# Layer 1 attention: the rotary step and the hi/lo split done in the projection's PSUM bank, row maxima over single banks in a ring of three

## What is computed

```
q, k, v = x @ wq.T, x @ wk.T, x @ wv.T           # (4, 1024, 512) each, as 16 heads of 32
q, k = apply_rope(q, k, sin, cos)                # rotates the first 16 of the 32 columns of a head
att = softmax(q k^T / sqrt(32))                  # over the 1024 keys of the batch entry
y = (att v).reshape(4, 1024, 512)
```

## Time and profile before

| | us |
|---|---|
| median of three runs | 3529.43 (3527.44 to 3536.01) |
| the profiled execution, its own time | 3538.25 |
| its span in the profile | 3536.5 |
| PE, PEld busy | 3178.8, 2231.9 |
| DVE, ACT, POOL busy | 2400.1, 1662.3, 1501.5 |
| mean granted TensorE clock | 0.96 |

### The profile page before, as it was taken

The page is one execution under the profiler, slowest core; times in us unless marked ns, Lnnn a source line. Parts: engine busy times, 40 slices in busy tenths (PEclk is TensorE's granted clock), DMA queues, the critical chain, the costliest instruction groups (busy, mean ns, idle before and its releaser), DMA issues. The chain is left out here.

```text
span 3536.5 us, 53506 instructions
## 1 busy us (share of the span) xinstructions
PE 3178.8 (90%) x16548; PEld 2231.9 (63%) x16548; DVE 2400.1 (68%) x3422; ACT 1662.3 (47%) x3006; POOL 1501.5 (42%) x1085
## 2 busy tenths in 40 slices
PE   5999999919999996999999989999999939999999
PEld 4766666617888885655555555555555418888887
DVE  4455555478888884788888888888888844444444
ACT  2211121106777774566666666666666622222222
POOL 1000000033333331377777777777777732112111
PEclk9999999959999998899999999999999969999999
DMA  2000000031222223111111111111111032122121
GB/s 83 25 24 24 30 24 24 18 113 66 90 89 89 89 78 127 60 51 54 54 55 55 54 55 50 54 54 49 54 55 54 20 150 75 60 74 68 65 74 48
DMA packets 97104, 215.26 MB, mean 61 GB/s; under 512 B 11408, under 2 KB 27792, under 8 KB 96400
## 3 DMA queue, kind: packets, MB, share of 16 engines
q1 hardware_dynamic: 95472, 210.14, 17.6%
q10 hardware_dynamic: 1440, 2.76, 0.2%
HBM read 162.54 MB, written 50.33 MB: 60 GB/s over the span
## 5 line engine op out<-in xcount | busy, mean ns | idle before, releaser
L1102 POOL TENSOR_TENSOR l_attn_summed<-l_attn_summed,l_attn_probs 128x1024 f32<-128x1024 f32 x372 | 884.8, 2402 | 161.0 <-ACT l_attn_probs L1170 160.7
L1259 DVE TENSOR_REDUCE l_attn_maxima<-l_attn_ps_max 128x2 f32<-128x1024 f32 x512 | 608.9, 1210 | 127.9 <-PE l_attn_ps_max L1367 125.3
L1170 ACT ACTIVATE l_attn_probs<-l_attn_ps_sc 128x512 f32<-128x512 f32 x1024 | 578.7, 601 | 217.7 <-PE l_attn_ps_sc L1323 200.2
L1323 PE MATMUL l_attn_ps_sc<-l_attn_q_st,l_attn_k_st 128*128 128x512 f32 x1024 | 451.9, 454 | 15.4 <-ACT l_attn_probs L1170 12.6
L70 PE MATMUL l_ffn_ps_gu<-l_ffn_w_gu,l_ffn_xt 128*128 128x512 f32 (+1 forms) x1536 | 345.6, 378 | 47.0 <-DMA l_ffn_xt<-xt_chunks 47.0
L1367 PE MATMUL l_attn_ps_max<-l_attn_k_st,l_attn_q_st 96*128 96x512 f32 x1024 | 352.9, 428 | 28.4 <-DVE l_attn_maxima L1259 28.3
L1510 POOL TENSOR_TENSOR l_ffn_mixed<-l_ffn_gate,l_ffn_up 128x512 f32<-128x512 f32 (+1 forms) x96 | 115.2, 1199 | 522.6 <-DVE l_ffn_up L1559 519.0
L70 PEld LDWEIGHTS l_ffn_ps_gu<-l_ffn_w_gu,l_ffn_xt 128*128 128x128 f32 x1536 | 279.7, 189 | 87.6 <-DMA l_ffn_xt<-xt_chunks 48.7
L1323 PEld LDWEIGHTS l_attn_ps_sc<-l_attn_q_st,l_attn_k_st 128*128 128x128 f32 x1024 | 193.9, 194 | 222.0 <-ACT l_attn_probs L1170 139.1
L1308 PE MATMUL l_attn_ps_y<-l_attn_probs,l_attn_v 128*32 128x512 f32 x2048 | 286.1, 632 | 16.5 <-issue 12.3
L61 PE MATMUL l_attn_ps_prep<-l_attn_wqkv_hi,l_attn_xt 128*128 (+1 forms) x1016 | 271.2, 348 | 31.8 <-DMA l_attn_xt<-xt_chunks 30.9
(11 more groups left out here) (232 smaller groups left out, 6584.7 us busy)
## 6 DMA issues: line engine op xcount, KB each, us to landing
l_attn_xt<-xt_chunks SPq DMA_DIRECT2D x128, 512.0 KB, 3.3
xt_chunks<-l_ffn_xt SPq DMA_DIRECT2D x32, 512.0 KB, 2.8
l_ffn_xt<-xt_chunks SPq DMA_DIRECT2D x32, 512.0 KB, 3.4
l_attn_xin<-in_x SPq DMA_DIRECT2D x32, 256.0 KB, 2.7
s<-l_attn_s_sb SPq DMA_DIRECT2D x32, 256.0 KB, 2.0
l_ffn_xa<-in_x SPq DMA_DIRECT2D x32, 256.0 KB, 2.6
l_ffn_xb<-in_x SPq DMA_DIRECT2D x32, 256.0 KB, 2.9
l_ffn_s_sb<-s SPq DMA_DIRECT2D x32, 256.0 KB, 3.6
```

Source lines behind the costliest of these rows:

```text
L1102: eng.tensor_tensor(total[:, :, :], old[:, :, :], probs[u % RING][:, :, :], ALU.add).then_inc(adds_with(g, u)[0], 1)
L1170: act.activation(probs[u % RING][:, i, :], ps_sc[i][:, :, :].rearrange("p a n -> p (a n)"), ACT.Exp, scale=ATT_SCALE).then_inc(exp_done, 1)
L1259: dve.tensor_reduce(maxima[:, j, h:h + 2, half:half + 1], ps_max[bank][:, :, :], AX.X, ALU.max).then_inc(max_read[bank], 1)
L1323: pe.matmul(ps_sc[i][:, :, :].rearrange("p a n -> p (a n)"), k_st[p][:, h, P * kt:P * kt + P], q_st[p][:, h, DIM * qb:DIM * qb + DIM], sta ...
```

## The change

1. **Banks.** `ps_max` goes from two tiles of two banks to three of one bank. The bank that comes free is `ps_proj`, for projections alone; `ps_prep` keeps q, k, den and turn. `ps_y` is declared in another shape.
2. **The rotary step in PSUM.** ACT no longer copies q and k out; it copies v alone. DVE waits for that copy, forms the two sine products into `swapped`, waits for them, multiplies by the cosines in place in `ps_proj`, and adds `swapped` in place. `turned_part` and `qk` are gone. ACT's `cast` and DVE's two subtractions read the bank. The next projection waits until both subtractions of the chunk before have been done (`stacked`).
3. **The table.** `PREP_AT` becomes `(1, 6, 7)`: projection c in slot 3 of unit 2c, its q in slot 1 and its k in slot 3 of unit 2c+3. ACT's `cast` of chunk c goes from unit 2c+2 to unit 2c+1. DVE does step 2 at the head of its unit in place of the end. "turn" is one unit earlier (units 30 and 14 in place of 31 and 15), "den" one unit later.
4. **The maxima.** 64 uses of one matmul and one reduce over 512 columns in place of 32 of two matmuls and one reduce over 1024, one to a slot.
5. **In tick 0**, which has no attention half, projections use `ps_proj` and the two `ps_sc` in turn, the other preps `ps_prep` and `ps_y`.
6. SP's loads of `xt` wait for the projection itself, no longer for ACT's copy.

```diff
-    MAX_RING = 2
+    MAX_RING = 3
-        ps_prep = ps("ps_prep", [P, 4, P])
-        ps_max = [ps(f"ps_max{i}", [P, 2, DIM]) for i in range(MAX_RING)]
+        ps_proj, ps_prep = ps("ps_proj", [P, 4, P]), ps("ps_prep", [P, 4, P])
+        ps_max = [ps(f"ps_max{i}", [P, DIM]) for i in range(MAX_RING)]
-        N_MAX = CPB * HPG // 2
-        PREP_STEP, PREP_AT = 4, (0, 7, 9)
-        DEN_AT = [2 * (LAST + 5), 2 * 7]
+        N_MAX = CPB * HPG
+        PREP_STEP, PREP_AT = 4, (1, 6, 7)
+        DEN_AT = [2 * (LAST + 6), 2 * 8]
-        EARLY = 7
+        EARLY = 14
-        TURN_AT = [2 * (UNITS - 1), 2 * (LAST - 1)]
+        TURN_AT = [2 * (UNITS - 2), 2 * (LAST - 2)]
...
+        def proj_bank(m, c):
+            banks = [ps_proj] + ps_sc if isinstance(m, int) and m == 0 else [ps_proj]
+            return banks[c % len(banks)], CPB * m + c - len(banks) + 1
... sync
-                        need(sp, qk_copied, CPB * m + c - 1)
+                        need(sp, proj_done, CPB * m + c - 1)
... scalar: cast reads bank[:, 0, :] and bank[:, 1, :] in place of x
-                    if u >= 2 and u % 2 == 0 and u // 2 <= CPB and live(m, NT):
-                        cast(m, p, u // 2 - 1)
+                    if u % 2 == 1 and u // 2 < CPB and live(m, NT):
+                        cast(m, p, u // 2)
...
+                        if kind == "proj":
+                            need(act, proj_done, CPB * m + c + 1)
+                            act.activation(v[p][:, c, :], proj_bank(m, c)[0][:, 2, :], ACT.Copy).then_inc(v_copied, 1)
+                            continue
... vector, chunk
-                    need(dve, qk_copied, n + 1)
-                    (cosine product into turned_part, two sine products into swapped)
+                    need(dve, v_copied, n + 1)
+                    dve.tensor_tensor(swapped[:, :, 0:R // 2], x[:, :, R // 2:R], sc(sin_t, 0, R // 2), ALU.mult).then_inc(rope_step, 1)
+                    dve.tensor_tensor(swapped[:, :, R // 2:R], x[:, :, 0:R // 2], sc(sin_t, R // 2, R), ALU.mult).then_inc(rope_step, 1)
+                    need(dve, rope_step, S * n + 2)
+                    dve.tensor_tensor(x[:, :, 0:R], x[:, :, 0:R], sc(cos_t, 0, R), ALU.mult).then_inc(rope_step, 1)
                 elif step == 1:
                     need(dve, rope_step, S * n + 3)
+                    dve.tensor_tensor(x[:, :, 0:R], x[:, :, 0:R], swapped[:, :, :], ALU.add).then_inc(rope_step, 1)
... tensor, prepare and maximum
+                    bank, free = proj_bank(m, c)
+                    need(pe, stacked, 2 * free)
-                for i in range(2):
-                    (matmul of head h + i into dst[:, i, :])
+                pe.matmul(dst[:, :], q_st[b][0:AUG, h, P * j:P * j + P], k_st[b][0:AUG, h, DIM * half:DIM * half + DIM],
+                          start=True, stop=True).then_inc(max_done[bank], 1)
+                    per_slot = -(-len(todo) // 4)
-                        for e in todo[slot // 2::2] if slot % 2 == 0 else []:
+                        for e in todo[per_slot * slot:per_slot * (slot + 1)]:
```

More of the change, by code:

```diff
@@ L1060, in ring @@
             of_tick = lambda m: [e for e in uses if exists(m, e)]
-            before = lambda m: sum(len(of_tick(i)) for i in range(m))
-            assert len(uses) % banks == 0
+            on = lambda n, bank: (n - bank + banks - 1) // banks
             def use(m, e):
                 if isinstance(m, int):
[L1066 to L1069, removed]
+                    n = of_tick(m).index(e)
+                    return n % banks, sum(on(len(of_tick(i)), n % banks) for i in range(m)) + n // banks
+                n = uses.index(e)
+                first = sum(on(len(of_tick(i)), n % banks) for i in range(2))
+                return n % banks, on(len(uses), n % banks) * (m - 2) + first + n // banks
             return use
-        prep_use = ring([e for u in range(UNITS) for e in preps(u) if e], 1)
+        prep_use = ring([e for u in range(UNITS) for e in preps(u) if e and e[0] != "proj"], 1)
         max_use = ring([e for u in range(UNITS) for e in maxes(u)], MAX_RING)
         def prep_bank(m, e):
-            banks = [ps_prep] + ps_sc if isinstance(m, int) and m == 0 else [ps_prep]
+            banks = [ps_prep, ps_y] if isinstance(m, int) and m == 0 else [ps_prep]
             n = prep_use(m, e)[1]
             return banks[n % len(banks)] if len(banks) > 1 else ps_prep, n - len(banks) + 1
+        def proj_bank(m, c):
+            banks = [ps_proj] + ps_sc if isinstance(m, int) and m == 0 else [ps_proj]
+            return banks[c % len(banks)], CPB * m + c - len(banks) + 1
         def adds_with(g, u):
@@ L1149, in cast @@
                 n = CPB * m + c
-                x, qs, ks = qk[c % 2], q_tok[c % 2], k_tok[c % 2]
+                bank, qs, ks = proj_bank(m, c)[0], q_tok[c % 2], k_tok[c % 2]
                 if not (isinstance(m, int) and m == 0 and c < 2):
@@ L1258, in maximum @@
                 need(dve, max_done[bank], before + 1)
-                dve.tensor_reduce(maxima[:, j, h:h + 2, half:half + 1], ps_max[bank][:, :, :],
+                dve.tensor_reduce(maxima[:, j, h, half:half + 1], ps_max[bank][:, :],
                                   AX.X, ALU.max).then_inc(max_read[bank], 1)
@@ L1280, in tick @@
                     for c in range(CPB):
+                        if u == PREP_STEP * c // 2 + 2 and live(m, NT):
+                            chunk(m, p, c, 2)
                         if u == PREP_STEP * c // 2 + 1 and live(m, NT):
@@ L1287, in tick @@
                         maximum(m, a)
-                    for c in range(CPB):
-                        if u == PREP_STEP * c // 2 + 2 and live(m, NT):
-                            chunk(m, p, c, 2)
                     for qb in range(QB):
@@ L1304, in pv @@
                 need(pe, exp_done, 2 * (UNITS * g + 2 * j + 2))
+                y = ps_y[:, :, :].rearrange("p a n -> p (a n)")
+                if isinstance(g, int) and g == 0 and j == 0:
+                    need(pe, prep_read, prep_use(0, ("turn", 0))[1] + 1)
                 if kt == 0:
@@ L1336, in prepare @@
                     three_pass(pe, bank[:, 0:3, :].rearrange("p a n -> p (a n)"), lambda k: xt[b][:, 0, k, :], lambda k: xt[b][:, 1, k, :],
[L1337 to L1338 removed]
+                               cols(w_hi), cols(w_lo), KD, proj_done)
+                    return
+                bank, read_before = prep_bank(m, e)
+                need(pe, prep_read, read_before)
+                if kind == "den":
                     for pair in range(2):
```

49 lines of the change are left out of this document (17 added, 32 removed).

## The result

| | before | after |
|---|---|---|
| median, us | 3529.24 (3527.44 to 3536.01) | 3782.54 (3778.47 to 3793.26) |
| profiled execution, its own time | 3538.25 | 3779.89 |
| its span | 3536.5 | 3778.1 |
| mean granted TensorE clock | 0.96 | 0.94 |

The ratio is 1.0719, with a 95% interval of 1.0691 to 1.0746: 7.2% slower, 253 us. Forecast were 3773 us and "slower". Between the two profiled executions the difference is 242 us; the one of the kernel before was 9 us slower than its median, the one of the kernel after 3 us faster.

The account below looks back on a forecast made before the run. No engine is free, so the waits of PE, which runs in order, were taken to count. 15 ticks x (10 us waits + 6 us clock) + 4 us for tick 0 = 244 us, giving 3773 us; range 3625 to 3865.

Parts of the forecast that it names:

- The wait's size: PE's wait for k in units 3, 5, ... 15: seven a tick, 2.2 us each, 2.4 without maxima.
- The chain: From PE's start behind a projection, through rotary step, casts and q's copy, until k may start: 3.65 us.
- rival 3: ACT reaches q's copy early, so no wait for k; chain under 2.3 us; 120 us faster, 3410 us; chance 0.08.
- rivals 3 and 4: Besides rival 3, the fourth: chain of about 2.3 us without clock loss, near no change, 3520 to 3540 us; chance 0.04.
- two over-counts named as the likeliest: If k's waits were under 1 us: the chain's maximum (0.60 us) and DVE's wait on its own result (0.22 us).
- The clock: TensorE's lower level after six more waits a tick, 1.5 us each: 0 to 9 us, two thirds taken, 6 us.
- Rival 1: The waits for k come but the clock holds: 154 us longer, 3683 us; chance 0.22.
- rival 2: Every wait for k is followed by TensorE's lower clock level: 289 us longer, 3818 us; chance 0.21.
- SP's earlier loads can only help: SP's loads of xt at a tick: no cost expected; the wait for xt of 0.64 us comes once a tick.
- Tick 0: The tick without attention: q's copy stands behind a cast, some 0.5 us for eight chunks, 4 us longer.
- The maxima: DVE's 64 single reduces: 2 us a tick more of DVE; possible cost to PE without projections 0 to 1 us.
- The turn's wait: In unit 15 q's transposes wait for ACT's copy of the turn; its removal is worth 2.4 + 1.5 us.

Follow-up runs that it names:

- e1: The changed kernel with ACT copying q's transposes out of ps_prep ahead of the cast in each unit: 3565.44 us, ratio 1.0091 to the kernel before.
- e3: The changed kernel with q's four transposes repeated five more times by PE inside the wait for k, chunks 0 to 6: 3703.96 us, ratio 1.0478.
- e2: The changed kernel with SP's store of y's first half issued behind the next tick's first two loads of xt: 3736.97 us, ratio 1.0589.
- e5: The kernel before with the change's single-bank row maxima alone, as a ring of four banks: 3520.56 us, ratio 0.9959.
- e4: The changed kernel with the rotary step and split back in SBUF, ACT again copying q and k out: 4050.99 us, ratio 1.1464.
- e7: The changed kernel with the edits of e1 and e2, and ACT's copy of ps_y ahead of the cast in unit 1: 3515.82 us, ratio 0.9946.

## Why the prediction came out

The direction and the cause were right by the mechanism. That the number came within 10 us is in part luck: of the 16 us a tick, and of the 4 us of tick 0, several terms were off and cancel. Point by point, by its own steps:

- **The main mechanism** is shown. k waits for q's copy, which stands behind a cast that needs the rotary step of a projection just done. e1 undoes that order alone and takes 217 of 253 us away.
- **The wait's size.** Forecast were seven waits of 2.2 to 2.4 us; the tick above has eight, seven of 1.6 to 2.5 (mean 1.9) and one of 0.86 in unit 17, 14.1 us in all as against about 16 and half a microsecond. The chain was 0.4 us too long: 0.19 by DVE's wait on an own result, 0.10 by ACT's start behind PE, 0.09 by the casts, 0.07 by the sine products. Even at 3.22 it stays well above the 2.3 us at which rival 3 decides, so rivals 3 and 4 fall. Of the two over-counts named as the likeliest, the wait on an own result was one, and the maximum, which is there, was not.
- **The clock.** Forecast were 6 us a tick, between 0 and 9; PE's busy time grew by 75 us over the kernel before, 5.0 a tick, e3 gives 5.3 at least, and e1's gain beyond its waits is 96 us, 6.4 a tick. The two thirds were a guess: half of the waits for k are followed by the lower level, and the late `xt` adds some. Rival 1, no clock loss, is refuted; rival 2's premise, that every wait is followed by it, is too, and its 9 us is more than e1 gave back at a granted clock of 0.99.
- **Two terms were missing.** "SP's earlier loads can only help" is the step that failed: the loads stand behind a store that the change made later; e2 puts that at 45 us. And the second copy of `ps_y` stands behind the new cast in unit 1, 0.98 us a tick. They make good what the chain was too long by, so that the sum fits better than its terms. In the tick above, the stretch from the first projection to the end of unit 15 (2092.33 to 2157.34) takes 65.0 us, 13.2 more than before, where 10 + 6 were forecast; the rest of the tick takes 41.0, 2.9 more, where nothing was.
- **Tick 0** has the wrong sign: 4 us longer was forecast. From its first projection to the first score of tick 1 it takes 52.2 us after the change and took 56.3 before, 4.1 us less. The forecast counted only q's copy behind a cast, and nothing for the three banks that projections have there or for the earlier turn; which of these makes the gain was not tried. (The first and last line of it, before and after, stand below the list.)
- **The maxima** had the wrong sign, as far as e5 shows: 0 to 1 us a tick were put down as a possible cost, and e5 gained 12 us in all in the kernel before, with a ring of four. In the changed kernel, with its ring of three, they were not tried alone.
- **DVE in PSUM.** 0.29 us for each 128-column instruction was right (0.28 to 0.30 for the cosines, the add and both subtractions). The 65 ns more for a PSUM source, an estimate from the cycle table in the errata section of the Trainium skill's page "VectorE: DVE Perf Modes", don't show: k's subtraction takes 279 ns from PSUM in the kernel after and 282 from SBUF, undisturbed, in e4. Leaving it out of the sum was right.
- **The turn's wait** is gone: behind 2149.31 PE goes on with maxima.
- **The part without projections** was to stay near 37 us and is 40.4. The cut moved with the turn, so it now holds the last projection (2.2 us) and two waits for k (1.57 and 0.86); it isn't the same work as in the earlier trace rows.
- **DVE's busy time** fell by 251 us with a longer span, as foretold.

Tick 0, before and then after:

```profile
1397.52 1.01 PE L61 MATMUL l_attn_ps_prep<-l_attn_wqkv_hi,l_attn_xt 128*128 128x384 f32 x2 [22.21 <-DMA l_attn_xt<-xt_chunks]
...
1453.84 0.79 PE L1323 MATMUL l_attn_ps_sc<-l_attn_q_st,l_attn_k_st 128*128 128x512 f32 x1 [1.16 <-ACT l_attn_q_st L1191]
```

```profile
1399.40 1.01 PE L61 MATMUL l_attn_ps_proj<-l_attn_wqkv_hi,l_attn_xt 128*128 128x384 f32 x2 [22.30 <-DMA l_attn_xt<-xt_chunks]
...
1451.62 0.80 PE L1331 MATMUL l_attn_ps_sc<-l_attn_q_st,l_attn_k_st 128*128 128x512 f32 x1
```

The accounts close roughly: 253 us, less 217 by e1, less 50 by e7's further two orders, leaves 14 us faster than before. e5's 12 us could be that, the turn's wait too; this rest wasn't taken apart.

## What to carry to other kernels

Before moving a use of a shared buffer, write down the whole chain that its release now depends on, with everything that stands ahead of it in each engine's list; here one copy behind a cast cost 6%, and the same change with three positions in the lists moved is 1.4% faster than before. An engine's busy time can fall by 250 us and the program still get slower, so forecast from the waits of the engine that bounds, and after each repair look for the new wait in the same bank. A stage's stores and loads that one engine issues in order belong in that chain: a producer made later holds up the loads behind its store.

## What the runs showed of the hardware

- DVE and POOL: in e4 a 128x128 add of DVE with both inputs in SBUF that starts while a POOL add runs ends 0.14 to 0.15 us behind that add (52 of 52, up to 2.39 us), and one that starts while POOL has none running takes 0.28 to 0.29 (32 of 32). With one input in PSUM it takes 0.29 to 0.30 either way (kernel after). q's subtraction, which writes to SBUF, does the same: 1.67 to 1.83 us in 22 of 84 cases in e4, and at most 0.29 in the kernel after, so one input in PSUM is enough. The sine products, the cosines and k's subtraction of e4 read SBUF alone too and stay at 225, 217, 291 and 282 ns: none of them starts inside a POOL add there. In the kernel before some do, and the means are 345, 233, 599 and 817.
- The granted clock: recurring waits of PE of about 1.8 us, one in each 7 to 10 us of the part with projections, go with 0.92 in the stage; the same stretch with those waits filled or more than halved has 0.98 or 0.99. About half of these waits (40 of 81) were followed by the lower level. Redundant matmuls made the kernel 79 us faster.
- A wait of DVE on a result of its own last instruction showed as 0.04 us between the two here, as against 0.22 in the earlier trace rows.
